# Two masked pairs' low parts made by two transfers, and a step's beta products laid between the next step's first-layer tiles

## The reference

```python
logits = _gelu(xf @ w_r1 + b_r1) @ w_r2 + b_r2
top_p, top_i = jax.lax.top_k(softmax(logits), 2)          # 2 of 8 experts for each token
v = 0; integrated = xf
for _ in range(2):
    ctx = concatenate([integrated, v])
    shared_ctrl = _gelu(ctx @ w_s1 + b_s1) @ w_s2 + b_s2  # D -> 3 D: alpha, beta, gate
    x_shared, v_shared = _inl(shared_ctrl, integrated, v, mu)
    hidden = _gelu(ctx @ expert_w1[i] + b1[i])            # 64 wide, for each chosen expert
    ctrl = hidden @ expert_w2[i] + b2[i]                  # 3 D wide: alpha, beta, gate
    x_r, v_r = _inl(ctrl, ...)                            # weighted by the two shares, summed
    x_next, v_next = mix of shared and expert results
    halt = sigmoid(_gelu(x_next @ w_h1 + b_h1) @ w_h2 + b_h2)
    refined = _gelu(x_next @ w_f1 + b_f1) @ w_f2 + b_f2
    integrated = integrated + halt * refined * integration_weight
    v = v_next
# _inl: v_next = sigmoid(alpha) v - softplus(beta) (x - mu); x_next = x + 0.1 sigmoid(gate) v_next
```

## Time and profile before

| | |
|---|---|
| median of 3 runs | 353.13 us (353.09 to 355.68) |
| the profiled execution, its own time | 352.54 us |
| its span, first to last instruction | 350.8 us |
| PE busy | 320.6 us, 91% |
| DVE busy | 276.4 us, 79% |
| ACT busy | 194.8 us, 56% |
| POOL busy | 35.4 us, 10% |
| mean granted clock of PE | 0.981 |

### The profile page before, as it was taken

The page is one execution under the profiler, slowest core; times in us unless marked ns, Lnnn a source line. Parts: engine busy times, 40 slices in busy tenths (PEclk is TensorE's granted clock), DMA queues, the critical chain, the costliest instruction groups (busy, mean ns, idle before and its releaser), DMA issues.

```text
span 350.8 us, 4318 instructions
## 1 busy us (share of the span) xinstructions
PE 320.6 (91%) x1498; PEld 225.9 (64%) x1498; DVE 276.4 (79%) x548; ACT 194.8 (56%) x307; POOL 35.4 (10%) x41
## 2 busy tenths in 40 slices
PE   4989999899898777896998999999999999999996
PEld 4654787445464454574675777777777777776763
DVE  0556767645757668969999999999997996999694
ACT  3500026285746274497778784866746846635743
POOL 0040020211111110709000100000000000000000
PEclk9989999999999679999999999999999999999999
DMA  7999930000000000000000100101000100000001
GB/s 266 421 429 298 325 153 0 0 2 2 0 2 0 0 1 2 0 0 2 1 0 0 33 0 2 30 0 30 2 1 0 32 1 0 32 0 0 32 0 60
DMA packets 11444, 18.91 MB, mean 54 GB/s; under 512 B 416, under 2 KB 8864, under 8 KB 10144
## 3 DMA queue, kind: packets, MB, share of 16 engines
q1 hardware_dynamic: 10848, 17.60, 14.5%
q0 software_dynamic: 576, 1.05, 1.8%
HBM read 16.55 MB, written 1.05 MB: 50 GB/s over the span
## 4 chain that ended last, share of the span: by engine, by line
PE 68%; DVE 15%; ACT 7%; issue 5%; POOL 2%; DMA 2%; SPq 0%; DVEq 0%; ACTq 0%; POOLq 0%
PE ps L1255 63%; DVE zz L860 3%; POOL lrs L381 2%; DVE lst L845 2%; PE ps L1352 2%; DMA ctxT<-in_ctxT 2%; PE ps L1331 1%; ACT hid L535 1%; DVE st L745 1%; ACT ring L483 1%; ACT L646 1%; DVE lmv L848 1%; DVE a L761 1%; PE ps L1437 1%; DVE kv L1144 1%
## 5 line engine op out<-in xcount | busy, mean ns | idle before, releaser
L1255 PE MATMUL ps<-hm_even,ew_hi 128*128 128x512 f32 (+1 forms) x160 | 51.0, 417 | 1.1 <-issue 1.1
L1255 PE MATMUL ps<-hm_odd,ew_hi 128*128 128x512 f32 (+1 forms) x164 | 51.6, 416 | 0.0
L1255 PEld LDWEIGHTS ps<-hm_odd,ew_hi 128*128 128x128 f32 (+1 forms) x164 | 28.7, 189 | 5.8 <-issue 0.5
L1255 PEld LDWEIGHTS ps<-hm_even,ew_hi 128*128 128x128 f32 (+1 forms) x160 | 27.9, 188 | 6.3 <-issue 1.2
L535 ACT ACTIVATE hid<-ps,pB 128x512 f32<-128x512 f32 x32 | 21.6, 687 | 13.4 <-PE ps L1255 12.8
L1255 PE MATMUL ps<-hm_odd,ew_lo 128*128 128x512 f32 (+1 forms) x80 | 28.3, 391 | 0.0
L1255 PE MATMUL ps<-hm_even,ew_lo 128*128 128x512 f32 (+1 forms) x80 | 28.3, 390 | 0.0
L860 DVE TENSOR_SCALAR zz<-ps,lmv,lrs 128x128 f32<-128x128 f32 x48 | 16.4, 404 | 9.4 <-POOL lrs L381 9.2
L381 POOL TENSOR_TENSOR lrs<-lve,mhalf 128x4 f32<-128x4 f32 x12 | 12.2, 1017 | 106.0 <-DVE lve L850 106.0
L1255 PE MATMUL ps<-x_hi,w1x_hi 128*128 128x512 f32 x40 | 18.9, 474 | 4.3 <-ACT ring L503 2.2
L945 DVE SCALAR_TENSOR_TENSOR ring<-ring,pB,hid 128x1024 f32<-128x1024 bf16 x16 | 20.5, 1282 | 2.0 <-ACT hid L535 1.3
(11 more groups left out here) (291 smaller groups left out, 739.4 us busy)
## 6 DMA issues: line engine op xcount, KB each, us to landing
ring<-in_fc1b SPq DMA_DIRECT2D x4, 1024.0 KB, 17.8
ring<-in_fc2a SPq DMA_DIRECT2D x4, 1024.0 KB, 8.9
packC<-in_packC SPq DMA_DIRECT2D x1, 1152.0 KB, 9.3
pB<-in_packB SPq DMA_DIRECT2D x1, 1141.5 KB, 10.1
ctxT<-in_ctxT SPq DMA_DIRECT2D x2, 512.0 KB, 6.7
xtok<-in_xtok SPq DMA_DIRECT2D x1, 1024.0 KB, 9.4
xT<-in_xT SPq DMA_DIRECT2D x1, 1024.0 KB, 11.4
a<-in_fc1a SPq DMA_DIRECT2D x1, 1024.0 KB, 13.4
```

The costliest lines, as they stand in the source:

```text
L1255: return pe.matmul(out, lhsT, rhs, start=start, stop=stop)
```

## The change

In steps 1, 2 and 3 (`MOVED`) DVE makes no low part for the pairs 2 and 3. It writes the **negated** high part (`tensor_scalar` by -1 in place of the cast). SP copies this to the place of the low part (512 KB, SBUF to SBUF), and when that has landed POOL adds `hm[j % 2]` to it by an accumulating transfer (512 KB): hm - high. The high products of these pairs use negated weights, `ew2_neg` and `ew2_low_neg`, two new tiles that ACT fills by two copies of 128x768 in the attention stage (t == 2); they lie where the context was, so the router's `r1` goes to another place and its memset of ones comes later on POOL. `hm` of the next step waits for these transfers (`low_ready`). `weigh(2)` goes behind POOL's two transfers of step 1, and the four accumulating transfers of `xi` behind all six new ones, on one semaphore in order.

`hidden_masked(1)` gets an order of its own, with `state_split(2)` and `slot_masks(2)` late in it and kept(1, 3) before them. In `controls` the products are split into `high(i)` and `low(i)`; in BETA of step 1 the lows of tiles 3 to 6 all stand behind the highs. On PE only the tiles 0 and 1 of hidden(s + 1) stand ahead of BETA in steps 1 and 2; `hidden_rest` (tiles 2, 3 and HT) goes ahead of tile 5 in step 1 (behind two products with no use, `busy(2, ...)`) and ahead of tile 3 in step 2, with refine_b(0).

```diff
+        MOVED = (1, 2, 3)
+        def lowered(s):
+            return {0: (1, 2, 0, 3), 1: (1, 0)}.get(s, (0, 1) if s in MOVED else (0, 1, 2, 3))
...
+        def negated(s, j):
+            return s in MOVED and j >= 2
+        def low_ready(engine, s, j):
+            if negated(s, j):
+                engine.wait_ge(sem(f"hlo_{j}"), 16 * (MOVED.index(s) + 1))
+            else:
+                engine.wait_ge(sem("hlo"), hlo_at(s, j))
...
@@ sync
+            for n, s in enumerate(MOVED):
+                for j in (2, 3):
+                    sp.wait_ge(sem("hhi"), hhi_at(s, j))
+                    sp.dma_start(low_of(s, j).bitcast(F), high_of(s, j).bitcast(F)).then_inc(sem("low"), 16)
+                    sp.wait_ge(sem("low"), 16 * (2 * n + j - 1))
@@ gpsimd
-            weigh(2)
+            for n, s in enumerate(MOVED):
+                for j in (2, 3):
+                    pool.wait_ge(sem("low"), 16 * (2 * n + j - 1))
+                    pool.dma_start(low_of(s, j), hm[j % 2], accum_op=ALU.add).then_inc(sem(f"hlo_{j}"), 16)
+                if s == 1:
+                    weigh(2)
@@ scalar, t == 2
+                    for out, w in ((ew2_neg, ew2_hi), (ew2_low_neg, ew2_lo)):
+                        act.activation(out[:, :], w[:, 2 * 3 * D:].bitcast(F), ACT.Copy, scale=-1.0)\
+                            .then_inc(sem("ew2_neg"), 1)
@@ vector
+            def high(s, j):
+                if s >= 2:
+                    dve.wait_ge(sem("part_ps"), group(s - 1, 0))
+                dve.wait_ge(sem("hm"), (HT - 1) * s + j)
+                if negated(s, j):
+                    dve.tensor_scalar(high_of(s, j), hm[j % 2], -1.0, None, ALU.mult).then_inc(sem("hhi"), 1)
+                else:
+                    dve.tensor_copy(high_of(s, j), hm[j % 2]).then_inc(sem("hhi"), 1)
...
+                if s == 1:
+                    kept(s, 2)
+                    high(s, 2)
+                    lower(s, 1)
+                    kept(s, 3)
+                    high(s, 3)
+                    lower(s, 0)
+                    state_split(s + 1)
+                    slot_masks(s + 1)
+                    shared_halves(s)
+                    return
+                kept(s, 1)
                 kept(s, 2)
+                if s in MOVED:
+                    high(s, 2)
                 if next_state:
                     state_split(s + 1)
                 lower(s, 0)
                 lower(s, 1)
                 kept(s, 3)
-                lower(s, 2)
+                if s in MOVED:
+                    high(s, 3)
+                else:
+                    lower(s, 2)
                 if s <= 2:
                     slot_masks(s + 1)
                 shared_halves(s)
-                lower(s, 3)
+                if s not in MOVED:
+                    lower(s, 3)
@@ tensor, controls
+                late = s == 1 and rows_last
+                for i in (1, 3, 5, 2, 4, 6) if n == LAST else range(1, NT):
+                    if i in between:
+                        between[i]()
+                    high(i)
+                    if i < 3 or not late:
+                        last = low(i)
+                if late:
+                    for i in range(3, NT):
+                        if 10 + i in between:
+                            between[10 + i]()
+                        low(i)
@@ tensor, steps
+                def hidden_rest():
+                    if s == 1:
+                        pe.wait_ge(sem("squash"), 4)
+                        busy(2, bank[0])
+                    hidden(s + 1, (2, 3, HT))
+                    if s == 2:
+                        refine_b(s - 2)
-                if s + 1 < STEPS:
+                if s <= 2:
+                    hidden(s + 1, (0, 1))
+                elif s + 1 < STEPS:
                     hidden(s + 1)
-                if s >= 2:
+                if s >= 3:
                     refine_b(s - 2)
-                controls(s, BETA, between={1: {2: expand_3, 5: weights_1}, 2: {3: weights_2, 6: weights_3}}.get(s, {}))
+                controls(s, BETA, between={1: {5: hidden_rest, 6: expand_3, 13: weights_1},
+                                           2: {3: hidden_rest, 5: weights_2, 6: weights_3}}.get(s, {}))
```

More of the change, by code:

```diff
@@ L176, in build @@
         xi = sb("xi", [128, T])
-        r1 = ctxT[0:33, 0:2 * CH].rearrange("p (a n) -> p a n", a=2)
+        r1 = a1_f[0:33, 0:2 * CH].rearrange("p (a n) -> p a n", a=2)
         lg = sb("lg", [128, B, E])
@@ L224, in build @@
         ws2_lo = sb("ws2_lo", [128, 3 * D], FR)
+        ew2_neg, ew2_low_neg = (nc.alloc_sbuf_tensor_at(n, [128, 2 * 3 * D], FR, offset=ctxT_at + 4 * i * 6 * D)
+                                for i, n in enumerate(("ew2_neg", "ew2_low_neg")))
         W1C = 2 * E * H + 4 * H
@@ L271, in hid_at, with hhi_at @@
             return HT * s + order(s).index(j) + 1
+        MOVED = (1, 2, 3)
+        def lowered(s):
+            return {0: (1, 2, 0, 3), 1: (1, 0)}.get(s, (0, 1) if s in MOVED else (0, 1, 2, 3))
         def hlo_at(s, j):
-            return HT * s + ((3, 1, 2, 4)[j] if s == 0 else j + 1)
+            return sum(len(lowered(r)) for r in range(s)) + lowered(s).index(j) + 1
+        def hhi_at(s, j):
+            return (HT - 1) * s + ((2, 1, 3) if s in MOVED else (1, 2, 3)).index(j) + 1
+        def negated(s, j):
[5 more added lines that the diff above has]
+                engine.wait_ge(sem("hlo"), hlo_at(s, j))
         def router_bank(c):
@@ L943, in kept @@
                 elif s >= 1:
-                    dve.wait_ge(sem("hlo"), HT * s - (j - 1))
+                    low_ready(dve, s - 1, 2 if j == 2 else 3)
                 dve.scalar_tensor_tensor(hm[j % 2], idx[:, c, :, :], W("tile_expert", j, j + 1),
@@ L1605, in controls, with high, low @@
                     shared(False)
-                for i in (1, 3, 5, 2, 4, 6) if n == LAST else range(1, NT):
+                def high(i):
                     j, k = TILES[i]
-                    if i in between:
-                        between[i]()
-                    pe.wait_ge(sem("hlo"), hlo_at(s, j))
+                    pe.wait_ge(sem("hhi"), hhi_at(s, j))
                     out = hi if k else lo
-                    mm(out, weights(ew2_hi, j), m[:, 0, i, :], start=rows_last and j == 1, stop=False)
-                    mm(out, weights(ew2_lo, j), m[:, 0, i, :], start=False, stop=False)
-                    last = mm(out, weights(ew2_hi, j), m[:, 1, i, :], start=False,
+                    if negated(s, j):
+                        pe.wait_ge(sem("ew2_neg"), 2)
+                        w_hi, w_lo = weights(ew2_neg, j - 2), weights(ew2_low_neg, j - 2)
+                    else:
+                        w_hi, w_lo = weights(ew2_hi, j), weights(ew2_lo, j)
+                    mm(out, w_hi, m[:, 0, i, :], start=rows_last and j == 1, stop=False)
+                    mm(out, w_lo, m[:, 0, i, :], start=False, stop=False)
+                def low(i):
+                    j, k = TILES[i]
+                    low_ready(pe, s, j)
+                    last = mm(hi if k else lo, weights(ew2_hi, j), m[:, 1, i, :], start=False,
                               stop=not rows_last and j == HT - 1)
```

45 lines of the change are left out of this document (26 added, 19 removed).

## The result

| | before | changed |
|---|---|---|
| median, 22 runs each on one chip | 355.43 us | 351.28 us |
| lowest and highest | 352.44 to 357.29 | 350.31 to 355.27 |
| the profiled execution, its own time | 352.54 us | 350.56 us |
| its span | 350.8 us | 348.7 us |

The ratio is not that of the two medians, which would be 0.988: the runs lie in two groups, and the medians fall into different ones. The forecast was a median of 350.4 us. The medians differ by more (4.15 us) than the profiled executions do (1.98 us); the part on the prediction comes back to that.

What follows compares the result with a forecast made beforehand. PE was taken to bound the kernel, only its stalls before 203.92 us counting. Gains of 1.55 in step 1 and 1.1 in step 2, 2.65, say 2.7, took 353.13 to 350.4 us; 8-in-10 range 348.6 to 353.2.

Steps and rivals of the forecast that it cites:

- what it called no difference: Whole kernel: about 1% (3.5 us) can be told from no change, so the forecast 0.8% gain counted as within 1%.
- gain by the end of BETA(1): PE in step 1: new stalls of 2.55 us against 4.1 before, a gain of 1.55.
- gain of step 2: PE in step 2: the 1.42 us wait of hidden(3)'s third tile filled, a new 0.3 at weights_3; gain 1.1.
- negated high to landed low, pair 3 of step 1: Chain of copy and accumulation with issue and signals: 9.4 us, between 6.7 and 14.8.
- copy: 512 KB within SBUF, no row: taken as 3.2 us, between 2.3 and 6.7, as the queues are empty then.
- room in step 1 (DVE at kept(2, 1)): Low part of high(1, 3) lands at 167.3, DVE wants it at 171.35: slack 4.0 us.
- room in step 2 (PE at tile 5): Low part of high(2, 3) lands at 189.2, PE wants it at about 192.2: slack 3.0 us, the smallest.
- The sum: Gains of PE in steps 1 and 2 together: 2.65 us, with rounding 2.7.
- DVE must keep up: DVE in step 2: slot_masks(3) done at 180.4, PE wants them at 182, slack 1.6 us.
- The transfers: Low parts of steps 1 to 3 through two queues: cost nothing up to a chain of 12.4 us.
- What is moved past: weigh(2), xT additions, ACT's negations and r1 memset, moved or added: cost nothing, at worst 0.5 us for the negations.
- The clock: Rival: PE's clock falls in step 1's new stalls, 168.1 to 170.8, costing 1.7 us: 352.1; chance 0.11.

Runs made afterwards that it cites:

- a0: The changed kernel once more, no edit, beside the kernel before: 351.01 us, ratio 0.9919.
- no_busy: The changed kernel without the two products of no use ahead of tile 2 of hidden(2): 351.28 us, ratio 0.9952 against the kernel before.
- b0: The kernel before once more, no edit: 355.66 us, ratio 1.0015.
- pe_order: The changed kernel with only PE's new order kept: DVE's old order, low parts on DVE, no transfers; 353.35 us, ratio 0.9976 against the kernel before.
- no_pe_order: The changed kernel with PE's old order; transfers and DVE's order as changed: 357.78 us, ratio 1.0076 against the kernel before.
- dve_low: The changed kernel without the transfers, DVE making all low parts in the new order: 350.39 us, ratio 0.991 against the kernel before.
- dve_low_fill: dve_low plus products of no use, eight ahead of hidden(0) and four ahead of expand_3: 353.65 us, ratio 0.9961 against the kernel before.
- v1_dve: dve_low with expand_3 behind the lows of tile 4 and weights_1 behind BETA(1)'s shared part: 350.04 us, ratio 0.9896 against the kernel before.
- before_fill: The kernel before plus eight products of no use in PE's 2.18 us wait for the masks: 352.8 us, ratio 0.9973.
- copies2: The changed kernel with each SP copy made twice in sequence: 352.04 us, one run.
- copies3: The changed kernel with each SP copy made three times in sequence: 366.82 us, one run.

## Why the prediction held in its sum and failed in what it called no difference

Term by term (times in us; an idle time in a trace is 0.16 less than the stall that I summed):

| step of the prediction | forecast | trace |
|---|---|---|
| tile 0 of hidden(2) behind GATE(0) | 160.75 | 160.78 |
| its third tile | 165.1 | 165.26 |
| HT | 166.9 | 166.98 |
| `expand_3`, idle ahead of it | 169.25, 0.94 | 169.34, 0.93 |
| `weights_1`, idle ahead of it | 0.51 | 0.43 |
| gain by the end of BETA(1) | 1.55 | 1.53 |
| gain of step 2 | 1.1 | 2.52 - 1.53 = 0.99 |
| stepped(0), stepped(1) begin | 162.6, 183.8 | 162.74, 184.15 |
| masks for step 3 done | 180.4 | 180.66 |
| negated high to landed low, pair 3 of step 1 | 9.4 | 11.1 |
| the same, the other five | 9.4 | 7.7 to 9.4 |
| copy | 3.2 | 2.9 to 4.1, and 5.5 |
| accumulation | 5.5 | 4.5 to 5.9 |
| room in step 1 (DVE at kept(2, 1)) | 4.0 | 2.5 |
| room in step 2 (PE at tile 5) | 3.0 | 3.6 |

*The sum* was right: 2.65 forecast, 2.52 in the stretch. The parts and their places are those of the text. At the end of the span 2.1 of it are left. *DVE must keep up* was right, and its slack of 1.6 came out as 1.5 (180.66 against 182.13). *The transfers* cost nothing in the stretch, as forecast, but one term of their chain was mis-sized. The copy was taken as 3.2 "as the queues are empty then"; in step 1 the kernel's own accumulation of pair 2 was in them, and the copy of pair 3 took 5.5 (5.8 in a0, 5.7 in no_busy). So the smallest room is DVE's in step 1, 2.5, and not PE's in step 2.

The rule of the Trainium skill, "SBUF — State Buffer", section "SBUF: two separate sides", that descriptors wait for DVE's two-port mode, was taken to make the chain up to 11.9. The page has the wait end with DVE's instruction, and the casts and `tensor_scalar` here last 0.69 at most, so by that rule too 2.5 was too much. The rows show issues of 0.85 to 1.07 us. Accumulations with no copy beside them landed in 4.5 to 5.2 beside a busy DVE. The 5.9 of the first one is the only longer one, and there a copy ran beside it; a delay by DVE can't be told from that.

*What is moved past* cost nothing in the stretch: no wait there is ended by `weigh(2)` or by the additions to xT. ACT's negations took 1.56 together (95.05 to 96.61), and step 0 begins its `expand` at 158.17 in both traces.

*The clock* didn't fall in step 1 in two traces of the changed kernel. Over the traces with their transfers on time the pattern is this: of the four with a wait of 2.0 or more in step 1 (the first of before, b0, pe_order, no_pe_order) all but the first have a fall there, and of the eight without it (the changed kernel, a0, no_busy, dve_low, dve_low_fill, v1_dve, before_fill, copies2) none has. So the rival had the sign wrong: the fall goes with the wait that the change removes, not with the new ones. It made b0's stretch 0.68 longer, and may be a part of what the medians gain beyond the traces; that is argued from one trace each. The highest runs of the changed kernel still reach 355, as those of before do, and dve_low's trace, one of the long ones, has its lateness ahead of step 0.

**The step that failed** is the one sentence on what can be told: "A measurement of this kernel can tell about 1% (3.5 us) from no change". From it came the weight of 0.66 on no difference. The interval of 22 runs each has a half width of 0.27%, and 0.7% is well outside it. The text gives no source for its 1%; the only spread it had was that of three runs, 2.6 us. What a comparison tells is given rather by the spread over the root of the number of runs. A forecast of 0.8% was a forecast of a faster kernel.

**A second reading was too short.** The 353.13 of three runs wasn't the middle of the kernel before: 22 runs gave 355.43. Its runs lie in two groups, up to about 354 and from about 355 to 357.5, and in the first comparison 9 of the 22 are in the lower one. The changed kernel has 18 of its 22 below 353. The medians thus differ by 4.15 us, 2.5 from the stretch less 0.4 at the end, and the rest because more of its runs are in the lower group. Counted as the runs within 2 us of the lowest, it is 9 of 22 before and 13 of 22 changed, and with a0 11 of 17 and 9 of 12. There the medians differ by 2.32, so that rest came back at 0.2 only; its cause stays open. That the median came out only 0.9 above the forecast is in part luck: the base was 2.3 too low, and the medians moved by 1.4 more than the 2.7 forecast.

**Two more things the prediction passed over.** It priced the transfers at nothing and asked no further, while its own DVE sum, with 1.6 of slack in step 2 and stepped waiting for ACT, said that DVE had no need of them; dve_low has the whole gain. And it had no term for the end of the kernel, 0.4 us in each trace with the transfers.

## What to carry to other kernels

A wait on the critical engine goes only if the next producer in the chain is early as well: early masks alone moved 2.02 + 0.65 of waiting into 2.64 at the third tile, and work laid between alone left the 2.02. Price two such reorderings together and each alone. When an engine is relieved, ask first whether its slack was used up: 7.1 us less of DVE brought nothing here that the new order hadn't brought, and the transfers in its place cost 0.4. When transfers follow each other through two queues, lay them on one time line: the second copy met the first accumulation and took 5.5 in place of 2.9. And state what a comparison can tell from the spread and the number of its runs, not from the spread alone.

## What the runs showed of the hardware

Two executions of one program have the granted clock of 0.50 at different places: 130.00 to 145.00 at 0.97 in one and 0.89 in the other, 160.00 to 175.00 at 1.00 and 0.89. What a fall costs depends on what lies under it. The one at 127 was absent in dve_low_fill with no gain; the one between 135.5 and 139.5 in b0 goes with 1.6 us of lateness. Falls in step 1 came in three of four traces with a wait of 2.0 or more there and in none of eight without. In copies3 the clock was granted at 0.57 from 174 to 186, where PE had waited 6.74 until 179.41.

A copy of 512 KB within SBUF landed after 2.9 us when nothing ran beside it, and an accumulating one after 4.5 to 5.2, while 256 KB accumulated in 3.7. In step 1, where POOL's issue came 0.5 ahead of SP's, they took 5.5 and 5.9 (5.8 and 6.2 in a0); in step 3, where it came 2.7 ahead, 3.1 and 4.5. That they slow each other is the likely reading; no run moved them apart on purpose. A `tensor_scalar` that negates 128x1024 into fp32r takes the 0.69 of a cast. The kernels with twelve or more such transfers in steps 1 to 3 end 0.3 us later behind DVE's last instruction, 139 us after the last of the twelve; I have no explanation for that.
